# First layer of a two-layer graph network: its broadcast loads reshaped and moved to one queue, its message products padded to 128 rows, its per-group words packed

## The reference, cut to what matters

```
msg    = (s_n @ Ws_src)[src] + (s_n @ Ws_dst)[dst]        # and the same for the vectors
w1     = rbf @ W_rbf                                       # 16 numbers per edge -> 224 weights
m1     = tensor_product(msg, y, w1)                        # y: 4 numbers per edge
a      = sum(leaky(m1_s @ W_alpha) * alpha_dot)            # one logit per edge and head
val    = m1_s @ Ws_val, m1_v @ Wv_val, gated by a sigmoid
m2     = tensor_product(val, y, w2); h = m2 @ W_vlin
out    = segment_sum(softmax over dst of a * h)
```

## Time and profile before

| | |
|---|---|
| median of 3 runs | 12751.92 us (12701.03 to 12808.68) |
| the profiled execution | 12789.85 us, its span 12787.9 us |
| mean granted TensorE clock | 0.828 |
| busy, of the span | PE 80%, weight loads 59%, DVE 53%, POOL 46%, ACT 23% |
| DMA | 746309 packets, 1082.87 MB, mean 85 GB/s |
| queues | POOL's 385.65 MB, ACT's 362.01 MB, SP's 334.79 MB |

### The profile page before, as it was taken

The page is one execution under the profiler, slowest core; times in us unless marked ns, Lnnn a source line. Parts: engine busy times, 40 slices in busy tenths (PEclk is TensorE's granted clock), DMA queues, the critical chain, the costliest instruction groups (busy, mean ns, idle before and its releaser), DMA issues. The chain is left out here.

```text
span 12787.9 us, 231117 instructions
## 1 busy us (share of the span) xinstructions
PE 10188.7 (80%) x63264; PEld 7491.1 (59%) x63265; DVE 6748.7 (53%) x15624; ACT 2970.9 (23%) x8455; POOL 5936.0 (46%) x6293
## 2 busy tenths in 40 slices
PE   1588888888888888888888888887776588888888
PEld 1366666666666666666666666666655333333335
DVE  3444555454455455445555555554443477777775
ACT  0122222222222222222222222222222222222223
POOL 0344444444444444444444444444330277777774
PEclk7688888888888888888888888888775698898999
DMA  2233343333333333333333333333220022222221
GB/s 34 74 100 102 97 106 98 100 102 97 100 102 102 95 102 105 101 101 100 103 101 105 100 101 105 104 101 94 85 80 16 23 57 57 57 57 57 57 58 49
DMA packets 746309, 1082.87 MB, mean 85 GB/s; under 512 B 238169, under 2 KB 345049, under 8 KB 746274
## 3 DMA queue, kind: packets, MB, share of 16 engines
q0 software_dynamic: 225792, 385.65, 13.3%
q10 hardware_dynamic: 241638, 362.01, 9.1%
q1 hardware_dynamic: 278844, 334.79, 9.1%
HBM read 1065.92 MB, written 16.06 MB: 85 GB/s over the span
## 5 line engine op out<-in xcount | busy, mean ns | idle before, releaser
L737 PE MATMUL bank_pair<-w_msg,blocks 128*128 128x160 f32 (+3 forms) x15640 | 3300.8, 370 | 575.5 <-issue 535.7
L737 PEld LDWEIGHTS bank_pair<-w_msg,blocks 128*128 128x128 f32 (+2 forms) x15640 | 2705.7, 245 | 1336.3 <-issue 1295.9
L703 POOL TENSOR_TENSOR edge<-rbf,y 128x512 f32<-128x512 f32 x391 | 500.3, 1279 | 3724.8 <-PE bank_pair L725 3724.7
L782 PE MATMUL bank_pair<-w_val,vblocks 128*128 128x192 f32 (+1 forms) x12512 | 1929.0, 315 | 267.5 <-issue 229.4
L1391 POOL DMA_INDIRECT gotf<-f_tab,idx x1568 | 1696.7, 1082 | 746.0 <-issue 607.4
L782 PEld LDWEIGHTS bank_pair<-w_val,vblocks 128*128 128x128 f32 x12512 | 1867.8, 216 | 281.8 <-issue 256.3
L694 POOL DMA_INDIRECT got_src<-src_tab,idx x1568 | 1509.1, 962 | 726.6 <-POOL idx L688 367.5
L694 POOL DMA_INDIRECT got_dst<-dst_tab,idx x1568 | 1499.0, 956 | 529.3 <-issue 528.4
L1431 PE MATMUL bank_pair<-val,to_node 128*128 128x449 f32 x3136 | 1473.2, 618 | 3.0 <-DVE val L1534 3.0
L1046 DVE TENSOR_TENSOR vec<-bank_pair,y_edge 128x384 f32<-128x384 f32 x391 | 218.0, 558 | 2311.8 <-issue 901.7
L725 PE MATMUL bank_pair<-edge,w_edge 64*128 64x512 f32 x3128 | 966.0, 696 | 160.1 <-DVE blocks L1015 148.0
(11 more groups left out here) (258 smaller groups left out, 12668.1 us busy)
## 6 DMA issues: line engine op xcount, KB each, us to landing
y_wide<-in_y ACTq DMA_DIRECT2D x782, 256.0 KB
y_wide<-in_y ACTq DMA_DIRECT2D x782, 192.0 KB
rbf<-in_rbf SPq DMA_DIRECT2D x392, 256.0 KB
dst_bc<-in_dst_rows SPq DMA_DIRECT2D x391, 256.0 KB
y<-in_y SPq DMA_DIRECT2D x392, 128.0 KB
y<-in_y SPq DMA_DIRECT2D x392, 96.0 KB
got_src<-src_tab,idx POOLq DMA_INDIRECT x1568
got_dst<-dst_tab,idx POOLq DMA_INDIRECT x1568
```

Source lines behind the costliest of these rows:

```text
L703: pool.tensor_tensor(edge[slot][:], rbf8[slot][:], y8[slot][:], ALU.mult).then_inc(s["scaled"], 1)
L737: return nc.tensor.matmul(to, blocks[rows, k, P * t:P * t + P], w_msg[rows, c0:c1], start=start, stop=stop)
L782: last = nc.tensor.matmul(to[:, o0:o1], vblocks[:, k, e], w_val[:, c0:c1], start=n == 0, stop=n == 3)
```

## The change

Four things change together, all in the first layer.

1. The broadcast loads. Before, a load such as `y_wide[:, 0, :]` read an access pattern whose outer dimension was the row of y (4, 3 or, for rbf, the 8 repetitions). Now each load has an outer dimension of 16 or more: the repetition of 16 goes outside in `load_edge`, with another order of the rows in `rbf8`, `y8` and `w_edge`, and `load_wide` issues one DMA for each piece of 32 partitions. The bytes are the same. The DMAs per group go from 4 on SP and 5 on ACT to 18 on SP and none on ACT: 5 for the edge (rbf 3, y 2), 11 for the wide tiles, 1 `y_edge`, 1 `dst`.
2. SP's order in step g is new: wait for `value_out` of g-2 and issue `y_edge`; wait for `scaled` and load the edge of g+2; wait for `value_block` and load the wide tiles of g+1; wait for `far` and load `dst`.
3. `close_scalars` and `close_vectors` take all 128 rows of block 2. The added rows of `w_msg` are zero.
4. One word `marks` for each group packs this group's block, the block of the group before and that group's count of additional windows. DVE reads one word per step, PE and ACT one, and the branch is taken if the count is above zero. Only inside the branch is `more_from` read.

```
-    chain = Chain(dve, s["step"], 20)
+    chain = Chain(dve, s["step"], 22)
...
+def marks_of(eng, g):
+    mark = eng.value_load(marks[0:1, at_group(g)], min_val=0, max_val=2 ** 24 - 1)
+    return (nc.s_assert_within(mark & 255, 0, BLOCKS - 2), nc.s_assert_within((mark >> 8) & 255, 0, BLOCKS - 2), mark >> 16)
+def more_count(eng, g):
+    return eng.value_load(marks[0:1, at_group(g + 1)], min_val=0, max_val=2 ** 24 - 1) >> 16
-def more_of(eng, g, body):
-    first = eng.value_load(more_from[0:1, at_group(g)], min_val=0, max_val=MAX_W)
-    end = eng.value_load(more_from[0:1, at_group(g + 1)], min_val=0, max_val=MAX_W)
-    with eng.If(first < end):
-        body(first, end)
+def more_of(eng, g, count, body):
+    with eng.If(count > 0):
+        first = eng.value_load(more_from[0:1, at_group(g)], min_val=0, max_val=MAX_W)
+        body(first, first + count)
...
 def load_edge(g, slot):
     rows = group_of(A["rbf"], g)
-    y = group_of(A["y6"], g)
-    sp.dma_start(rbf8[slot][:], rows.unsqueeze(0).broadcast_to([8, NB, GE])).then_inc(s[f"edge{slot}"], 16)
-    sp.dma_start(y8[slot][0:64, :], y[0:4, :].unsqueeze(1).broadcast_to([4, NB, GE])).then_inc(s[f"edge{slot}"], 16)
-    sp.dma_start(y8[slot][80:128, :], y[1:4, :].unsqueeze(1).broadcast_to([3, NB, GE])).then_inc(s[f"edge{slot}"], 16)
+    y = group_of(A["y"], g)
+    for first, n in ((0, 4), (64, 1), (80, 3)):
+        r = slice(first, first + NB * n)
+        sp.dma_start(rbf8[slot][r, :], rows.unsqueeze(1).broadcast_to([NB, n, GE])).then_inc(s[f"edge{slot}"], 16)
+        if n > 1:
+            sp.dma_start(y8[slot][r, :], y[4 - n:4, :].unsqueeze(0).broadcast_to([NB, n, GE])).then_inc(s[f"edge{slot}"], 16)
+def load_wide(g, slot):
+    y = group_of(A["y"], g)
+    w = y_wide[slot]
+    for k, rows in ((0, range(4)), (1, (None, 2, 3, 1)), (3, (3, 1, 2, None))):
+        for q, row in enumerate(rows):
+            if row is not None:
+                sp.dma_start(w[32 * q:32 * q + 32, k, :], y[row, :].partition_broadcast(32)).then_inc(s[f"wide{slot}"], 16)
+        if k == 1:
+            sp.dma_start(w[:, 2, :], y[0, :].partition_broadcast(P)).then_inc(s[f"wide{slot}"], 16)
...
+    if late:
+        wait_apart(sp, s["value_out"], g * 2 - 2, s["tick_s"])
+    load_edge_y(g, slot)
     if not (isinstance(g, int) and g + 2 >= NG):
         wait_apart(sp, s["scaled"], g + 1, s["tick_s"])
         load_edge(g + 2, slot)
+    if not last_group(g):
+        if mid:
+            wait_apart(sp, s["value_block"], g * 2, s["tick_s"])
+        load_wide(g + 1, 1 - slot)
     if late:
         wait_apart(sp, s["far"], g, s["tick_s"])
     load_dst(g, slot)
...
 def close_scalars(t):
-    return add_piece(scalar_tile(t), 2, slice(96, P), t, 3, False, True)
+    return add_piece(scalar_tile(t), 2, slice(0, P), t, 3, False, True)
 def close_vectors(t):
-    add_piece(vectors[:, t, 0:96], 2, slice(0, 96), t, 2, False, False)
+    add_piece(vectors[:, t, 0:96], 2, slice(0, P), t, 2, False, False)
     return add_piece(vectors[:, t, :], 3, slice(0, P), t, 4, False, True)
...
-    act.dma_start(w[:, 0, :], y[0:4, :].unsqueeze(1).broadcast_to([4, 32, GE])).then_inc(s[f"wide{slot}"], 16)
-    act.dma_start(w[32:128, 1, :], y[2:5, :].unsqueeze(1).broadcast_to([3, 32, GE])).then_inc(s[f"wide{slot}"], 16)
-    act.dma_start(w[:, 2, :], y[0, :].partition_broadcast(P)).then_inc(s[f"wide{slot}"], 16)
-    act.dma_start(w[0:96, 3, :], y[3:6, :].unsqueeze(1).broadcast_to([3, 32, GE])).then_inc(s[f"wide{slot}"], 16)
-    act.dma_start(y_edge[slot][:], group_of(A["y_edge"], g)).then_inc(s[f"wide{slot}"], 16)
```

More of the change, by code:

```diff
@@ L178, in edge_rows @@
                 def edge_rows(half, k):
-                    return slice(64 * half + NB * k, 64 * half + NB * k + NB)
+                    if half == 0:
+                        return slice(k, 64, 4)
+                    return slice(79 + k, P, 3) if k else slice(64, 64 + NB)
                 put(w_edge[edge_rows(0, 0), 0, 0:32], Wr[:, o_ss:o_ss + 32])
@@ L533, in layer0 @@
             span_i = brief("span0_i", [1, NG_PAD], I32)
+            block_f = brief("block_f", [1, NG_PAD])
             scan_a = brief("scan_a0", [1, NG_PAD])
@@ L699, in combine @@
                 def combine(g, slot, use, fresh):
-                    wait(s[f"edge{slot}"], use * 48 + 48)
+                    wait(s[f"edge{slot}"], use * 80 + 80)
                     if not fresh:
@@ L833, in more @@
                                 wait_apart(pe, s["more_scaled"], w + 1, s["tick_p"])
-                        more_of(pe, g - 2, more)
+                        more_of(pe, g - 2, more_count(pe, g - 2), more)
                     if now:
@@ L917, in more @@
                                 wait_apart(act, s["more_added"], w + 1, s["tick_a"])
-                        more_of(act, g - 2, more)
+                        more_of(act, g - 2, more_count(act, g - 2), more)
                     if now:
@@ L949, in step @@
                         copy_turned(g + 1, False)
-                        if mid:
-                            wait_apart(act, s["value_out"], g * 2, s["tick_a"])
-                        load_wide(g + 1, 1 - slot)
-                load_wide(0, 0)
                 copy_turned(0, True)
@@ L982, in add_sums, with more_windows @@
                     return last
-                def more_windows(g, slot, b):
+                def more_windows(g, slot, b, count):
                     def body(first, end):
@@ L1003, in body @@
                             wait_apart(dve, s["more_added"], w + 1, s["tick_v"])
-                    more_of(dve, g, body)
+                    more_of(dve, g, count, body)
                 def step(g, slot, use, now, mid, late):
@@ L1017, in step @@
                     if mid:
-                        dve.wait_ge(s[f"wide{other}"], mid_use(slot, use) * 80 + 80)
+                        dve.wait_ge(s[f"wide{other}"], mid_use(slot, use) * 176 + 176)
                         if late:
@@ L1025, in step @@
                                               y_wide[other][:, 2 * half:2 * half + 2, :], ALU.mult).then_inc(s["value_block"], 1)
+                    if mid or late:
+                        now_block, b, count = marks_of(dve, g - 1)
                     if late:
-                        b = block_of(dve, g - 2)
                         dve.wait_ge(s["factors"], g - 1)
@@ L1032, in step @@
                         add_sums(b).then_inc(s["merged"], 1)
-                        more_windows(g - 2, slot, b)
+                        more_windows(g - 2, slot, b, count)
                     if mid:
@@ L1041, in step @@
                         dve.wait_ge(s["message"], g + 1)
-                        dve.wait_ge(s[f"wide{slot}"], use * 80 + 80)
+                        dve.wait_ge(s[f"edge_y{slot}"], use * 16 + 16)
                         if mid:
@@ L1069, in step @@
                             dve.wait_ge(s["factors"], g - 1)
-                        raise_peak(b, g - 1, (s["highest"], g * 4 - 4), (s["peak_kept"], g - 1) if late else None,
+                        raise_peak(now_block, g - 1, (s["highest"], g * 4 - 4), (s["peak_kept"], g - 1) if late else None,
                                    s["shifted"], s["rescale"]).then_inc(s["peak_kept"], 1)
```

26 lines of the change are left out of this document (14 added, 12 removed).

## The result

| | before | after |
|---|---|---|
| median of 8 runs | 12776.1 us | 12890.06 us (12870.21 to 12902.02) |
| ratio to before | | 1.0089, interval 1.0066 to 1.0113 |
| profiled execution's span | 12787.9 us | 12892.1 us |
| mean granted TensorE clock | 0.828 | 0.839 |

The change is 0.9% slower where it was measured first. Each time is therefore read against the kernel before on its own chip, and three kinds of chip are told apart by what the kernel before takes: the quick chips (7 and 14; 11,765 and 11,773 us), chip 11 (12,275 us, one run) and the slow chips (0, 1, 8, 10 and that of the result; 12,757 to 12,831 us).

What follows compares the result with a forecast made beforehand. PE was taken to bound an undisturbed group, with waits on top. Terms of 270 + 470 + 660 = 1,400 us off 12,790 gave 11,390, less 38 for the median: 11,350 us, range 10,750 to 12,080 (8 in 10).

Steps and rivals of the forecast that it cites:

- Packed words: On PE before the closing products, one of two reads goes: 0.7 us per group, 270 us in all.
- Padding: PE's closing stretch of 34 records gets shorter with 128 rows throughout: 1.2 us per group, 470 us in all.
- It all counts: Time saved before the closing products is on PE's own stream, so all 270 us come off; padding likewise PE's own time.
- The reshaped loads: Broadcast loads spread over more engines land sooner, so PE waits less: 1.7 us per group, 660 us in all.
- the 541 us at the logits: DVE's wait at L1065 in 197 of 391 groups, for something nameless; counted among the waits that reshaped loads could remove.
- the drain that I read in the earlier trace: DMA share falls from 0.41 to 0.00 after 6056 as DVE's late wait ends at 6055.48; taken as evidence for crowded loads.
- no more stretches near 0.2 at 74 GB/s: Sign in the profile after: the DMA share should lose these stretches, read as few engines working while others idle.
- the upper bound: Most the reshaped loads could bring: 2.8 us by which the mean group exceeds an undisturbed one of 20.67 us, 1,100 us.
- the clock's return: Rival: PE waits less in all groups and regains part of its half-clock time too; 10,340 us, chance 0.10.
- All from SP: SP issues 18 DMAs per step at 0.6 us each, 10.8 us within 19.8; nothing gained from relieving ACT.
- the hidden delay: Edge loads land some 2 us late for POOL's L703; POOL was idle 8.66 us, so 2 or 3 us stay hidden.
- the rival with SP as the bound: SP's chain of 18 DMAs at 1.32 us each takes 24.2 us per step with waits; 13,020 us, chance 0.06.

Runs made afterwards that it cites:

- experiment 1: Changed kernel with SP's edge loads ahead of its wait for value_out and y_edge: 0.8532 of the kernel before on quick chip 7, 0.9701 on slow chip 0.
- experiment 3: Kernel before with 128-row products and packed words, its own loads: 0.9845 and 0.9893 on quick chips 7 and 14, 0.9614 on slow chip 1.
- experiment 4: Kernel before with the reshaped loads, all from SP, edge loads first, no padding or packed words: 13248.39 us on slow chip 0, ratio 1.0337.
- experiment 6: Changed kernel, edge loads first, POOL's combine split so gathers no longer stand behind a wait for PE: 0.891 on quick chip 14, 1.0244 on slow chip 8.

## Why the prediction was wrong, by its own steps

**Packed words: right.** PE's idle time before the closing products fell from 1.41 us to 303.0/378 = 0.80; 0.6 us where 0.7 was put.

**Padding: right in size.** From the first closing product to L796 there are 4.18 us (7019.23 to 7023.41) where there were 5.15; 0.97 us at full clock, 1.07 was put. The rule of the Trainium skill that was weighed there ("TensorE: Matmul & The Clock Gate", Part 3) would have made the stretch 0.9 us longer; the trace is against it for these pieces.

**"It all counts": wrong by a third and more.** The two are PE's own time, but were worth 485 us of 740 on the slow chip and 136 to 181 on the quick ones. On the quick chips `y_edge`'s landing set the end again (1787.0 us of waits). On the slow chip the earlier message moved the value products in among the gathers: the last gather of a step was issued 2.9 us after the message's use before, and 7.4 us after it with PE's two parts alone (medians over the groups from 3000 to 6000 us, as all such figures below). With reshaped loads, on chip 0, the same parts brought 822 us. The terms don't add; each is worth more once the other is there.

**The reshaped loads: +660 us was put; this term failed most, downwards on slow chips and upwards on quick ones.** On the slow chips, where the forecast was measured, the loads brought nothing (times of two chips, 0 and 1, set side by side by their ratios): with SP's order as before they took some 110 us away on top of PE's parts (experiments 1 and 3), and alone they cost 431 us (experiment 4). The wrong step is the reading of the 541 us at the logits. I took them for the landing of crowded loads. But that wait went from 541.0 to 4.3 us with the old loads and PE's parts (experiment 3), and stood at 705.5 with the new loads without these parts (experiment 4). And the drain that I read in the earlier trace rows was not the loads': by the trace's packets POOL's queue, the gathers, has 0.38 of the 0.41 from 6055 to 6056, SP's queue 0.04 and ACT's nothing. In the place of crowded loads, the runs show PE's results waiting for gathers; on the kernel before itself this isn't tested by a run. The sign that I had named, no more stretches near 0.2 at 74 GB/s, told nothing: the window of 6043 in the earlier trace rows was ACT's loads alone (0.22 by the packets), and now the window 7030:7031 has 0.27 and 73, nearly all of it gathers.

On the quick chips the size was much too small. There the loads bring 11,628.82 - 10,050.92 = 1,578 us on top of PE's parts, over the 1,100 that I had called the upper bound. That bound compared the mean group with the undisturbed one of 20.67 us; but that one ran at 0.86 of the clock, so it wasn't undisturbed. A group without the waits stays at full clock and takes 16.2 us. The chance of 0.10 for the clock's return was too low: its 10,340 us are 0.811 of the median shown, and the quick chips gave 0.855 of theirs, below the 0.890 of the forecast. The waits for `y_edge` (1787.0 us in experiment 3) are gone there, which fits the Trainium skill's rule of an outer dimension of 16 or more ("DMA: Bandwidth & Descriptors", Rules for kernel authors). It doesn't prove it: the loads changed their queue and their order too, and no run parts these.

**All from SP: the cost per issue was right, the hidden delay was not.** In the step shown, SP's queue has:

```profile
7024.59 1.31 SPq L680 DMA_DIRECT2D y_wide<-in_y  x3
...
7036.44 0.57 SPq L670 DMA_DIRECT2D rbf<-in_rbf  x1
```

That is 0.44 and 0.57 us each, where 0.6 was put. SP is through with its loads at 7027.2 and waits 8.6 us for `value_out`, so the rival with SP as the bound falls. But this sentence fails: "POOL had been idle 8.66 us by then, and its results are needed one step later, so 2 or 3 us of delay stay hidden". The delay has the size: the product started 3.5 us after `value_out` and starts 6.3 us after it now (DVE's last value ends at 7035.66, the product starts at 7042.00). Its result is needed late, as I said. But I had counted only that product. Behind it in POOL's order stand the eight gathers, which moved too: in the step of the earlier trace rows the last was issued by 2.0 us after the message's use (6032.29 against 6030.31), now by 9.2 us after it (7032.81 against 7023.61). Most of this isn't SP's order: the medians are 2.9 us before, 7.4 with PE's parts alone, 7.4 with the edge loads first and 8.5 in the change. The order adds the last of it, and that is worth 472 us where the gathers hurt and nothing where they don't.

**What was not among the rivals: the gathers as the cause.** The whole loss against the quick chips, 12,882 against 10,051 us, is the gathers': with two of them the slow chip takes 10,043. The idle 5.07 us at the values and the half clock after it (0.86 over 23.55 us is 28% at half speed, worth 3.3 us) more than cover the 7.4 us between a group of 23.6 and one of 16.2; they overlap in part. The profile before held a sign of it that I read only half: the late group "comes free about when the transfers drain". I took the drain for crowded engines and put the gathers, "which end the drain too", aside as "not changed". Their bytes didn't change, but their place did.

So on slow chips the gain was given back as a new wait: PE's own two parts took the wait from the logits and brought the one at the values, and SP's order made it longer. That the forecast comes nearer on the quick chips (0.890 against 0.855) is in part luck, since its sum has PE's parts too large and the loads too small there.

**Open.** What inside the chip makes PE's results late while several gathers are in flight, and why only on some chips; whether it is the results or only the signal that they are there isn't told apart. It is not the bandwidth (73 to 77 GB/s in the windows above; the group on the quick chip has a mean of 144), nor the wide loads, nor slower gathers: by their packets the eight of a group take 9.6 us on the slow chip and 9.9 on quick chip 14 (medians). The kernel before with two gathers wasn't run on a slow chip, so how much of its own 12,790 us is the same hold-up isn't measured; nor was the change itself on chip 11. Nor were gathers spaced out in time, or the reshaped loads on ACT's queue.

## What to carry to other kernels

A wait that ends when the transfers drain doesn't say which transfers: take away one kind at a time before the wait is put down to one of them. A load that lands late isn't hidden because its consumer is idle: follow that engine's queue one step further, to what stands behind the consumer (here eight gathers), and ask what they will now run beside. An "undisturbed" group at a mean clock of 0.86 is not one; take as the bound what the engines' work takes at full clock. And a measurement on one chip is one sample: put the kernel before and the changed one side by side on more than one before a change of this size is believed or dropped. Here the version of experiment 1 is the one to keep if both kinds of chip count: 0.853 and 0.970. PE's two parts alone gave 0.961 on a slow chip, a little better, but only 0.985 and 0.989 on the quick ones.

## What the runs showed of the hardware

- The same kernel takes 10,051 us on one chip and 12,882 to 12,898 on others, each within 0.3%; the kernel before 11,765 to 11,773, 12,275, and 12,757 to 12,831. The difference lies in the stage with eight gathers per group (means of 16.5 and 23.7 us over 390 intervals), and is gone with two.
- On the slow chips, with eight gathers in a row, the last value products were usable 0.2 to 0.5 us after the gathers' last packet (medians of the change and of experiment 1) and 5 to 6 us after PE's last record of them. On quick chip 7 the same program used them 0.04 us after that record. The window sums of experiment 6 were 9.4 us late, and PE's own records then came 1.4 us apart. The gathers' issues keep their length (0.95 us).
- Going from pieces of 32 and 96 rows to 128 rows takes 0.97 us off 34 records with the same columns.
